# Two routed-expert products on the two row halves of the array, into two PSUM banks

## What is computed

```
x = x + 0.5 * ffn(layernorm(x))
x = x + attention(layernorm(x))      # 16 heads of 16 features, ALiBi bias, softmax over 512 keys
x = x + 0.5 * ffn(layernorm(x))
```

```
h = silu(x @ wg_r[e]) * (x @ wu_r[e])     # 256 -> 64
y = (h * share) @ wd_r[e]                 # 64 -> 256
```

## Time and profile before

| | |
|---|---|
| median of 3 runs | 2431.34 us (2420.27 to 2434.01) |
| the profiled execution | 2442.57 us, span 2440.8 us |
| TensorE matmul busy | 1838.3 us, 75% of the span |
| TensorE weight loads busy | 1217.7 us, 50% |
| VectorE busy | 1411.0 us, 58% |
| ScalarE busy | 1017.9 us, 42% |
| GpSimd busy | 940.8 us, 39% |
| mean granted TensorE clock | 0.845 of full speed |

### The profile page before, as it was taken

The page is one execution under the profiler, slowest core; times in us unless marked ns, Lnnn a source line. Parts: engine busy times, 40 slices in busy tenths (PEclk is TensorE's granted clock), DMA queues, the critical chain, the costliest instruction groups (busy, mean ns, idle before and its releaser), DMA issues.

```text
span 2440.8 us, 34106 instructions
## 1 busy us (share of the span) xinstructions
PE 1838.3 (75%) x10516; PEld 1217.7 (50%) x10516; DVE 1411.0 (58%) x3675; ACT 1017.9 (42%) x2015; POOL 940.8 (39%) x999
## 2 busy tenths in 40 slices
PE   4568885577889888878779777876888898845770
PEld 3455664354656565545445444544655565523550
DVE  5454445657655555567678777775565655563332
ACT  2224442244444444535445444543454554521330
POOL 3432325643432322153554455444233221254416
PEclk8777897888979898978899889988898998976685
DMA  6346663634775566644463546358475656449875
GB/s 181 110 139 210 186 211 125 132 87 96 215 189 150 159 160 176 151 129 86 94 135 88 89 106 134 84 94 257 126 184 142 190 148 155 142 128 300 269 256 155
DMA packets 313027, 376.46 MB, mean 154 GB/s; under 512 B 39304, under 2 KB 256008, under 8 KB 312840
## 3 DMA queue, kind: packets, MB, share of 16 engines
q1 hardware_dynamic: 276880, 289.84, 45.6%
q0 software_dynamic: 24576, 67.14, 10.0%
q10 hardware_dynamic: 11392, 17.31, 2.3%
HBM read 180.71 MB, written 146.80 MB: 134 GB/s over the span
## 4 chain that ended last, share of the span: by engine, by line
PE 45%; DVE 14%; DMA 13%; issue 9%; SPq 8%; another core or an unknown queue 4%; POOL 4%; ACT 2%; ACTq 0%; POOLq 0%; DVEq 0%
PE bank L986 7%; DMA den<-o_store 6%; PE bank L977 6%; PE bank L870 4%; PE bank L1080 4%; PE bank L872 4%; PE bank L871 4%; PE bank L1060 4%; PE bank L1027 3%; PE bank L1093 3%; PE bank L967 2%; SPq L818 2%; DVE den L1525 2%; DVE row_max L1428 2%
## 5 line engine op out<-in xcount | busy, mean ns | idle before, releaser
L1428 DVE TENSOR_REDUCE row_max<-bank 128x1 f32<-128x512 f32 (+2 forms) x768 | 349.2, 504 | 188.9 <-PE bank L1043 121.9
L1206 ACT ACTIVATE p_buf<-bank 128x512 f32<-128x512 f32 x640 | 361.3, 596 | 223.9 <-PE bank L1060 134.0
L1639 POOL TENSOR_SCALAR_AFFINE_SELECT p_buf<-p_buf 128x512 f32<-128x512 f32 x256 | 160.8, 642 | 420.8 <-ACT p_buf L1206 420.1
L1027 PE MATMUL bank<-k_stack,q_stack 99*128 99x512 bf16 (+3 forms) x1024 | 258.5, 323 | 78.3 <-issue 48.9
L1583 POOL DMA_INDIRECT sorted_x<-xn,position x256 | 250.4, 978 | 107.3 <-issue 69.5
L1060 PE MATMUL bank<-q_stack,k_stack 101*128 101x512 bf16 (+3 forms) x1024 | 244.6, 316 | 62.3 <-issue 18.3
L1605 POOL DMA_INDIRECT y_tok<-sorted_y,position x216 | 206.4, 956 | 192.0 <-DVE x_ffn L1495 65.1
L986 PE MATMUL bank<-t_w,t_h 64*128 64x256 f32 x752 | 244.4, 451 | 41.9 <-DVE t_h L1482 30.4
L977 PE MATMUL bank<-t_xt,t_w 128*128 128x256 f32 x752 | 237.3, 444 | 48.1 <-DMA t_w<-expert_w 32.6
L1080 PE MATMUL bank<-p_buf,v_rows 128*32 128x512 f32 (+3 forms) x2048 | 197.6, 488 | 15.0 <-POOL p_buf L1639 10.4
L986 PEld LDWEIGHTS bank<-t_w,t_h 64*128 64x128 f32 x752 | 142.7, 210 | 118.7 <-DVE t_h L1482 50.6
(11 more groups left out here) (165 smaller groups left out, 3591.4 us busy)
## 6 DMA issues: line engine op xcount, KB each, us to landing
t_w<-expert_w SPq DMA_DIRECT2D x188, 256.0 KB
t_x<-sorted_x SPq DMA_DIRECT2D x188, 256.0 KB
sorted_y<-t_y SPq DMA_DIRECT2D x188, 256.0 KB
q_stack<-qk_part SPq DMA_DIRECT2D x192, 128.0 KB
k_stack<-qk_part SPq DMA_DIRECT2D x192, 128.0 KB
sorted_x<-zeros SPq DMA_DIRECT2D x68, 256.0 KB, 3.6
o_store<-o_raw ACTq DMA_DIRECT2D x64, 256.0 KB
x_ffn<-in_L_attn_x SPq DMA_DIRECT2D x16, 512.0 KB, 4.9
```

Source lines behind the costliest of these rows:

```text
L1027: pe.matmul(ps[:, col:col + k1 - k0], q_stack[0:ROWS_S, h, P * qt:P * qt + P], k_stack[0:ROWS_S, h, k0:k1], start=(n == 0), stop=False, sk ...
L1206: act.activation(p_of(u), psum("score", *of)[:, :], ACT.Exp).then_inc(*exp_done.step(*of))
L1428: ins = dve.tensor_reduce(row_max[g % 2][:, n:n + 1], src[:, col:col + q1 - q0], X, ALU.max)
```

## The change

The two products of "tile out" no longer read the same 64 rows. The second product's tokens stand in partitions 64 to 127 of `t_h`, and it takes the second copy of `wd_r`, which is already loaded there. Each product writes a bank of its own.

```diff
-        def place(kind, who):
+        def place(kind, got):
...
-                if len(mine) >= self.limit(use):
+                if len(mine) + sum(what == kind for _, what, _, _ in got) >= self.limit(use):
                     return None
...
+                    if any(home == ("bank", i) for home, _, _, _ in got):
+                        continue
...
-        part(at + 0.6 * pace, "DVE", 0.84, hidden, (hidden, "ACT"))
-        part(at + 1.0 * pace, "PE", 1.1, made, (hidden, "DVE"), takes=[
-            bank("fill", ("ty", l, g, j), (made, "ACT"))], lag=0.3)
-        part(at + 1.0 * pace, "ACT", 0.6, made, (made, "PE"),
+        part(at + 0.6 * pace, "DVE", 0.98, hidden, (hidden, "ACT"))
+        part(at + 1.0 * pace, "PE", 0.65, made, (hidden, "DVE"), takes=[
+            bank("fill", ("ty", l, g, j, t), (made, "ACT")) for t in range(2)], lag=0.3)
+        part(at + 1.0 * pace, "ACT", 0.8, made, (made, "PE"),
...
-        t_h = [sb(f"t_h{i}", [ME, RT]) for i in range(2)]
+        t_g = sb("t_g", [ME, RT])
+
+        t_h = [sb(f"t_h{i}", [P, RT // 2]) for i in range(2)]
...
-                    pe.wait_ge(*th_step.at(*of, "u"))
-                    ps = take(("ty", *of), ty_out, *of)
+                    pe.wait_ge(*th_step.at(*of, "u", 1))
...
+                    halves = [take(("ty", *of, t), ty_out, *of, t) for t in range(2)]
                     for t in range(2):
-                        ins = pe.matmul(ps[:, D * t:D * t + D], hidden[:, P * t:P * t + P],
-                                        weights[0:ME, ND * P:ND * P + D], start=(t == 0), stop=(t == 1),
-                                        skip_group_check=True)
+                        at = slice(ME * t, ME * t + ME)
+                        ins = pe.matmul(halves[t][:, 0:D], hidden[at, :], weights[at, ND * P:ND * P + D],
+                                        start=True, stop=True)
...
-                    act.activation(t_y[i][:, :, :].rearrange("p t d -> p (t d)"), psum("ty", *of)[:, :],
-                                   ACT.Copy).then_inc(*ty_out.step(*of))
+                    for t in range(2):
+                        act.activation(t_y[i][:, t, :], psum("ty", *of, t)[:, 0:D], ACT.Copy
+                                       ).then_inc(*ty_out.step(*of, t))
...
-                    dve.scalar_tensor_tensor(t_h[i][:, :], t_th[:, :], 1.0, ps[0:ME, 0:RT], ALU.add, ALU.mult
+                    if before["t_th", *of]:
+                        dve.wait_ge(*th_step.at(*before["t_th", *of][1:], "u", 1))
+                    dve.scalar_tensor_tensor(t_g[:, :], t_th[:, :], 1.0, ps[0:ME, 0:RT], ALU.add, ALU.mult
                                              ).then_inc(*th_step.step(*of, "g"))
                     dve.wait_ge(*th_step.at(*of, "g"))
-                    dve.tensor_tensor(t_h[i][:, :], ps[ME:P, 0:RT], t_h[i][:, :], ALU.mult
-                                      ).then_inc(*th_step.step(*of, "u"))
+                    for t in range(2):
+                        at = slice(P * t, P * t + P)
+                        dve.tensor_tensor(t_h[i][ME * t:ME * t + ME, :], ps[ME:P, at], t_g[:, at], ALU.mult
+                                          ).then_inc(*th_step.step(*of, "u", t))
```

More of the change, by code:

```diff
@@ L192, in run @@
                     for what, who, freed in part[6]:
-                        home = place(what, who)
+                        home = place(what, got)
                         if home is None:
@@ L777, in do @@
                     i = index["t_y", l, g, j]
-                    sp.wait_ge(*ty_out.at(*of))
+                    sp.wait_ge(*ty_out.at(*of, 1))
                     sp.dma_start(sorted_y[l, g][RT * j:RT * j + RT].rearrange("(i p) d -> p i d", p=P),
@@ L973, in do @@
                     pe.wait_ge(*tx_out.at(*of))
-                    ps = take(("tgu", *of), th_step, *of, "u")
+                    ps = take(("tgu", *of), th_step, *of, "u", 1)
                     weights, xt = t_w[index["t_w", l, g, j]], t_xt[index["t_xt", l, g, j]]
```

## The result

The changed kernel takes 2362.21 us (median of 4 runs, 2358.15 to 2364.24) beside 2425.81 us for the kernel before (2410.47 to 2434.01): a ratio of 0.9743 with a 95% interval of 0.9688 to 0.9798. Measured again on another chip it was 0.9707 (0.9679 to 0.9735). The sign was as forecast, and so was what the pairing does to TensorE. The size was not: 1.4% was forecast, and 2.6 to 2.9% came.

The account below looks back on a forecast made before the run. TensorE, 45% of the chain, was taken to bound the kernel. Of 64 us saved on the chain 43 were kept, less 8 for VectorE: 35 us off 2431.34, 2396 us, 1.4% faster; range 2350 to 2443.

Parts of the forecast that it names:

- What the pairing saves on TensorE: Tile's second product: four passes take two pass times, 0.42 us less at full clock; 92 us of TensorE's time, 64 on chain.
- The rivals of the array: Second product's passes: one product's block the other's (2418 us, chance 0.12), or rows don't run side by side (around 2447, 0.08).
- The drain of a mode change: Borders of the 64-row products: 0.33 us gaps already there, nothing added; if new, 0.66 us a tile would undo the saving.
- How much of it stays: Chain after the saving: the next slowest path takes over, so two thirds of 64 us are kept, 43 us.
- The shares by stage: Chain saving in the three tile stages and the tail, before the discount: 14, 20, 19 and 11 us.
- What VectorE and ScalarE add: Split steps of tile out: VectorE 0.16 us more for about 50 of 188 tiles, 8 us; ScalarE's copies covered, nothing.
- The clock: Rival: with TensorE less busy the granted clock falls by 0.04, costing 26 us; 2422 us, no change; chance 0.08.
- the order of the work: Planner's order of pieces on the engines: no gain in the sum; a loss only in the rival of the banks.
- the rival of the banks: Tile out needs two of three fill banks at once, so tiles are held back 1.4 us each: 2452 us, chance 0.12.

Follow-up runs that it names:

- before_two_banks: Kernel before with its instructions and old costs, but the planner books two fill banks for each tile's second product (one used): 0.9889.
- after_old_costs: Changed kernel, planned with the old costs 0.84, 1.1 and 0.6 for the same pieces: 2374.53 us, 0.9744 to the kernel before.
- same_rows: Changed kernel with its order, two banks and split steps, but both products from partitions 0 to 63: 2420.5 us, 0.9923 to the kernel before.
- before_new_order: Instructions of the kernel before, one bank used and unsplit steps, in the order of the changed planner: 2407.65 us, 0.9878.
- after_again: Changed kernel, unaltered, measured once more beside the kernel before on another chip: 2367.14 us, 0.9707.
- the four nudges: Kernel before, one planned cost nudged in each: combine 3.4 us, first product 1.06, transposes 0.6, layer norm moments 2.2: 1.0063, 1.0021, 1.0014, 1.0008.
- before_nudge_flip: Kernel before, planned with 0.6 us instead of 0.65 for a tile's transposes: 1.0014.

## What of the prediction was right, and why its size was wrong

**What the pairing saves on TensorE: right.** 0.70 and 1.22 us were expected for the four passes, 0.70 and 1.23 came. The busy time was to be near 150 us and is 149.5. Reading the rows from the column strips held for rows too.

**The rivals of the array: wrong.** Passes of one product don't block those of the other: with three pass times in a row the four would have taken about 0.9 us. The Trainium skill, TensorE: Matmul & The Clock Gate, "Part 3: Packing small matmuls", has matmuls start in program order. The trace does not contradict that, if the two products' passes are issued in turns: it shows two starts 0.01 us apart, twice, but no row says which product a pass belongs to. The drain of a mode change (the Trainium skill, TensorEngine Tiling (Array Packing), "Key Properties") added nothing: the gap of 0.33 us is that of the earlier trace rows.

**How much of it stays: near, and perhaps too low.** I took 64 us on the chain and kept two thirds, 43. At one order the pairing measured 52 us (43 to 62), or 44 (29 to 59) by the changed kernel's first ratio, so a discount that was too large is not shown. The shares by stage were rougher: 14, 20, 19 and 11 us were forecast before the discount, and the traces of that order have 8, 28, 22 and 10, in two executions that lie 18 us further apart than the medians. At the second order (before_two_banks and after_old_costs, split steps included) they have a first stage 1 us longer and the others 11, 20 and 11 us shorter, so where the gain falls hangs on the order too.

**What VectorE and ScalarE add: not contradicted.** 8 us were charged, 11 measured (0 to 22), in the cheaper form of same_rows. The two halves take 0.62 us where 0.59 was expected, the two copies 0.66 where 0.75 was. TensorE's waits for `t_h` don't measure it: L992 has 38.7 us of them in one trace of the changed kernel and 56.6 in the other, beside 30.4 before. At the new order they are 25.2 us with whole steps (before_new_order) and 26.8 with split ones (same_rows), so most of the rise came with the pairing and not with the split.

**The clock: the rival was wrong.** The mean granted clock did not fall: the medians of after_again and of the kernel before beside it are 0.852 and 0.848. The rival's sum also took the 45% that TensorE has in the chain of the whole span for the four stages. There it has 57%, 59%, 55% and 42%, some 700 us and not 570.

**The step that failed is the order of the work**, to which the sum gave nothing and the rival of the banks only a loss. Booking two banks did not hold tiles back to any cost: before_two_banks is 1.1% faster, not slower. The changed planner's order is worth 30 us (21 to 38) with the instructions of before. The rest of the forecast, 43 - 8 = 35 us, stands beside 42 us (31 to 53) at this order and 35 (24 to 46) at the other. With the order's term the sum is 52 - 11 + 30 = 71 us, which is after_again's 2.9% by construction; the forecast had 43 - 8 + 0 = 35.

**What stays open.** Why these orders are better is not settled. Shown is that the four nudges do not do it (1.0063, 1.0021, 1.0014, 1.0008), that the lowest planned cost of the second product does most, and that two banks, new costs or a fourth bank each give 0.9 to 1.4% to the kernel before and don't add up. Whether these rules help by what they say or because any large move leaves a poor order is not shown. Nor is it shown whether the higher granted clock of some stages is a cause or follows from the order; it comes without any gain in before_nudge_flip.

## What to carry to other kernels

Where two products contract over 64 values or fewer and don't depend on each other, put their operands in the two halves of the partitions: here four float32 passes went from 1.13 to 0.70 us, TensorE's busy time fell by some 100 us, and the time by 44 to 52. Where an order is made by a planner, a change of its costs or buffers can move the time by itself, here by 0.1 to 2.3%, as much as the change one means to measure: hold the order still (same plan, old instructions) to read the mechanism, and try the plan's own numbers as a lever of their own. Here one of them, four banks instead of three, gave another 0.9% at no work.

## What the runs showed of the hardware that was not expected

The granted clock can rise when TensorE is given less to do: at one order it went from 0.87 to 0.90 over a stage in which TensorE's busy time fell from 512.15 of 594 to 475.13 of 566 us, 86% to 84%, though the first figure is from the run of same_rows with the lowest clock. Over all runs the median went from 0.848 (same_rows) to 0.852 (after_again). Busy share alone does not foretell the clock: the kernel before has 518.99 of 619 us in that stage, also 84%, and 0.86.

Two VectorE products of 64 partitions by 128 columns take 0.50 us as a pair when they work in place in the same 64 partitions, and 0.62 when they read a second tensor and the second writes the other 64 partitions; each is 289 to 294 ns long on average, so what is lost is the overlap. Which of the two differences does it was not tried apart.
